# Embeddings 4 to 10 from fp16 parts, and a new order of the work that follows the embeddings, in a one-core ViT block with a routed FFN

## The reference

```python
out = jnp.einsum('bnp,dp->bnd', patches, W) + b            # patches: 768 values each
h = concatenate([cls_tok, out])                            # 37 tokens per image
h = h + attention(layernorm(h), Wq, Wk, Wv, Wo, bo, betas, mem, z)
shared = silu(x_flat @ shared_w1.T) @ shared_w2.T          # x_flat = layernorm(h)
top_k_gates, top_k_idx = jax.lax.top_k(x_flat @ gate_w.T, 2)
h = h + shared + selected                                  # selected: 2 of 8 experts, weighted
```

## Time and profile before

| | us |
|---|---|
| median of 3 runs | 326.65 (326.32 to 326.92) |
| the profiled execution's own time | 325.89 |
| its span, first to last instruction | 324.0 |
| outside the span (325.89 - 324.0) | 1.89 |
| TensorE busy | 306.7 (95%) |
| VectorE busy | 223.4 (69%) |
| ScalarE busy | 184.5 (57%) |
| GpSimd busy | 152.1 (47%) |
| mean granted TensorE clock | 0.996 of 2.4 GHz |

### The profile page before, as it was taken

One profiled execution on the slowest core, in us unless ns is written; L12 is line 12 of the kernel. 1 busy time (PEld: TensorE's weight loads), 2 busy tenths in 40 slices (PEclk: granted clock), 3 DMA queues, 4 the chain that ended last, 5 costly groups with the idle time before them and its releaser, 6 DMA issues.

```text
span 324.0 us, 9888 instructions
## 1 busy us (share of the span) xinstructions
PE 306.7 (95%) x3521; PEld 259.6 (80%) x3521; DVE 223.4 (69%) x502; ACT 184.5 (57%) x355; POOL 152.1 (47%) x208
## 2 busy tenths in 40 slices
PE   8789999999998999999999999999999999999990
PEld 6678788988777999999997777777787787777870
DVE  0637888888898989999886868755554546565530
ACT  1366768878896978476768878733232332323220
POOL 0577747777586322112622344656353544434131
PEclk9999999999999999999999999999999999999998
DMA  7775335322241117814798774243323242333121
GB/s 231 260 222 210 108 111 179 111 83 77 77 124 58 32 31 205 269 24 95 195 275 309 185 239 110 45 67 41 60 42 59 34 67 35 54 48 46 22 34 16
DMA packets 18642, 36.37 MB, mean 112 GB/s; under 512 B 3331, under 2 KB 10982, under 8 KB 18598
## 3 DMA queue, kind: packets, MB, share of 16 engines
q1 hardware_dynamic: 12166, 27.71, 26.2%
q0 software_dynamic: 6432, 8.03, 16.3%
HBM read 28.52 MB, written 7.21 MB: 110 GB/s over the span
## 4 chain that ended last, share of the span: by engine, by line
PE 76%; DVE 9%; DMA 4%; POOL 3%; issue 3%; ACT 2%; SPq 1%; POOLq 1%; DVEq 0%; ACTq 0%
PE bank L820 21%; PE bank L833 14%; PE bank L643 7%; PE bank L835 6%; PE bank L500 6%; PE bank L602 6%; DMA out_rows<-y,add_id 2%; PE bank L525 2%; PE bank L551 2%; DMA weights<-in_patches 2%; PE bank L591 2%; PE bank L565 1%; PE bank L555 1%; DVE weights L1309 1%; PE bank L453 1%
## 5 line engine op out<-in xcount | busy, mean ns | idle before, releaser
L820 PEld LDWEIGHTS bank<-x_t,weights 128*128 x1248 | 87.5, 98 | 25.5 <-issue 0.2
L820 PE MATMUL bank<-x_t,weights 128*128 128x128 f16 x1248 | 103.8, 219 | 0.0
L1002 ACT ACTIVATE act_out<-bank 128x512 f32<-128x512 f32 (+2 forms) x72 | 42.0, 585 | 86.1 <-PE bank L820 71.8
L1270 POOL DMA_INDIRECT out_rows<-y,add_id x26 | 43.0, 1653 | 69.6 <-DVE y L1626 48.1
L833 PE MATMUL bank<-weights,hid_hi 128*128 x192 | 73.3, 382 | 0.2
L1417 DVE SCALAR_TENSOR_TENSOR hid_lo<-act_out,hid_hi 128x512 f16<-128x512 f32 (+2 forms) x72 | 48.6, 680 | 12.5 <-ACT hid_hi L1013 11.0
L835 PE MATMUL bank<-weights,hid_lo 128*128 x192 | 52.3, 273 | 0.0
L1423 DVE SCALAR_TENSOR_TENSOR weights<-stage,weights 128x1024 f16<-128x1024 f32 x36 | 43.0, 1221 | 0.7 <-ACT weights L959 0.7
L959 ACT ACTIVATE weights<-stage 128x1024 f16<-128x1024 f32 x36 | 36.8, 1049 | 0.0
L1237 POOL DMA_INDIRECT slot_rows<-x_rows,gather_id x26 | 28.0, 1075 | 13.0 <-DMA out_rows<-y 5.2
L500 PE MATMUL bank<-weights 128*111 128x256 f32 x132 | 31.3, 386 | 1.6 <-DMA weights<-in_patches 1.1
(11 more groups left out here) (164 smaller groups left out, 522.8 us busy)
## 6 DMA issues: line engine op xcount, KB each, us to landing
stage<-in_w_ffn SPq DMA_DIRECT2D x36, 512.0 KB
weights<-in_patches SPq DMA_DIRECT2D x11, 333.0 KB, 3.3
x_rows<-rows SPq DMA_DIRECT2D x11, 111.0 KB
out_rows<-weights SPq DMA_DIRECT2D x10, 111.0 KB
out_rows<-y POOLq DMA_DIRECT2D x9, 119.0 KB, 5.3
weights<-in_w_embed SPq DMA_DIRECT2D x3, 256.0 KB, 4.2
stage<-in_w_qk SPq DMA_DIRECT2D x1, 512.0 KB, 6.9
slot_rows<-x_rows,gather_id POOLq DMA_INDIRECT x26, 4.1
```

Source lines behind the costliest of these rows:

```text
L820: mm = nc.tensor.matmul(o, weights[:, bass.ds(base + 2 * k * CHUNK + 2 * (col - col % D) + w * D + col % D, P)], x_t[:, b, (2 * x + k) * P ...
L1002: nc.scalar.activation(d_, s_, ACT.Silu, scale=1.0 / (X_SCALE * W_SCALE)).then_inc(hid_acted, 1)
L1270: nc.gpsimd.indirect_dma_start(out=out, out_offset=bass.IndirectOffsetOnAxis(ap=add_id[:, j:j + 1], axis=0), in_=y[:, y_place(j)], in_offs ...
```

## The change

It has two parts.

**Embeddings from fp16 parts.** From tile 4 (`F16_FROM`) on, `embed` makes 18 fp16 matmuls (three products of parts, six pieces each) in place of six float32 ones. The parts have to be made:

- of the weight, once: ScalarE writes the hi parts (128x1024 and 128x512) ahead of its other work, VectorE the lo parts in step 1;
- of the patches, for each of the tiles 4 to 10: ScalarE writes 128x666 hi values (`split_patches_hi`, at the end of the steps 1 to 6, two of them in step 2), VectorE 128x666 lo values (`split_patches_lo`, in steps 1 and 2 late in the step, in steps 3 to 7 right behind `split_lo`).

`embed_h` scales the sum back in the instruction that adds the bias. The SP queue's loads of patches now wait for the split in place of the embedding. In steps 5 to 10 VectorE waits, ahead of `split_lo`, for `rstd2` of the pair that GpSimd began at the end of the step before.

**The joint.** `shared_up(0, 0)` is no longer one piece of 24 matmuls but four of six, put between other work. `row_lo` of the tiles 6 and 7 moves from VectorE to GpSimd. On ScalarE `exps(10)` now stands ahead of `norm2(7)`.

The core of the diff:

```diff
             def embed(t):
-                pe.wait_ge(patches_in[t % PATCH_RING], 16 * (t // PATCH_RING + 1))
+                if t < F16_FROM:
+                    pe.wait_ge(patches_in[t % PATCH_RING], 16 * (t // PATCH_RING + 1))
+                else:
+                    pe.wait_ge(patch_lo, t - F16_FROM + 1)
+                if t == F16_FROM:
+                    pe.wait_ge(we_lo, 2)
...
+                if t >= F16_FROM:
+                    for n, (x, w) in enumerate(EMBED_PRODUCTS):
+                        for k in range(PC):
+                            we = we_front[:, k, w] if k < 4 else we_back[:, k - 4, w]
+                            mm = nc.tensor.matmul(embed_bank(t), patch_pair[t % 2][:, x, k * T:(k + 1) * T], we,
+                                                  start=(n == 0 and k == 0), stop=(n == 2 and k == PC - 1))
+                    mm.then_inc(embed_ready, 1)
+                    return
...
             project_v(NT - 1)
+            shared_up(0, 0, (0,))
             project_out(NT - 4)
+            shared_up(0, 0, (1,))
             mix_values(NT - 3)
             turn_prob(NT - 2)
-            shared_up(0, 0)
+            shared_up(0, 0, (2,))
             turn_rows(NT - 5)
+            shared_up(0, 0, (3,))
...
+            def split_patches_hi(t):
+                act.wait_ge(patches_in[t % PATCH_RING], 16 * (t // PATCH_RING + 1))
+                if t >= F16_FROM + 2:
+                    act.wait_ge(embed_ready, t - 1)
+                nc.scalar.mul(patch_pair[t % 2][:, 0], s_patch[:, t % PATCH_RING].rearrange("p a b -> p (a b)"),
+                              P_SCALE).then_inc(patch_hi, 1)
...
+                if s in (1, 2):
+                    split_patches_hi(s + 3)
+                if 2 <= s < NT - 4:
+                    split_patches_hi(s + 4)
...
+            exps(NT - 1)
             norm2(NT - 4)
-            exps(NT - 1)
...
+                if s - 5 in POOL_LATE_ROWS:
+                    row_lo(s - 5)
...
+            def split_patches_lo(t):
+                dve.wait_ge(patch_hi, t - F16_FROM + 1)
+                nc.vector.scalar_tensor_tensor(
+                    out=patch_pair[t % 2][:, 1], in0=s_patch[:, t % PATCH_RING].rearrange("p a b -> p (a b)"),
+                    scalar=P_SCALE, in1=patch_pair[t % 2][:, 0], op0=ALU.mult,
+                    op1=ALU.subtract).then_inc(patch_lo, 1)
...
+                if s == 1:
+                    we_lo_of(0, we_front, s_we[:, 0:4])
+                    we_lo_of(1, we_back, s_we[:, 4:])
...
+                if 5 <= s < NT:
+                    dve.wait_ge(rstd2, s - 4)
                 for c in chunks_at(s):
                     split_lo(c)
+                if 3 <= s < NT - 3:
+                    split_patches_lo(s + 3)
                 if s + 2 < NT:
                     embed_h(s + 2)
+                if s == 1:
+                    split_patches_lo(4)
...
-            row_lo(NT - 4)
```

59 lines of the change are left out of this document (48 added, 11 removed).

## The result

The changed kernel takes 328.43 us (median of 4 runs, 328.03 to 328.83) against 326.76 us before, measured beside it: ratio 1.0061, 95% interval 1.0048 to 1.0073. The profiled execution took 328.03 us, its span 326.1. A second, later measurement gave 328.44 and a ratio of 1.0055 (1.0038 to 1.0072). It is slower, by 0.6%.

What follows compares the result with a forecast made beforehand. TensorE was taken to bound the 8.90 us step, a GpSimd ring 0.27 us short of it. 325.89 + 1.8 (to the embeddings' end) - 0.3 (joint) = 327.4 profiled, 328.1 us median; own range 327.2 to 328.9, 8 in 10 324.6 to 329.7.

Steps and rivals of the forecast that it cites:

- the block that holds GpSimd: VectorE's weight split and the new patch split behind it, during which GpSimd stands still: 1.22 + 0.74 = 1.96 us.
- The step of 8.90: Time from one weight split to the next in steps 5 to 8, 8.90 us before; forecast to become 9.36.
- the forecast picture: Steps 5 to 8: GpSimd's operation beside both splits over 2 us, `residual` waiting 0.8, TensorE waiting about 0.9 for `row_lo`.
- the rival "in between": GpSimd's `xln_lo` goes ahead of the weight split, its bias ahead of the patch split; step 9.74, median 329.2; chance 0.12.
- the path that was forecast: Steps 5 to 8: both splits 1.96, GpSimd to `row_lo` 1.92, to `residual` 1.37, statistics 1.10, pair 2.95, signal 0.06: 9.36 us.
- The wait: VectorE waiting for `rstd2` ahead of the weight split: about 0.1 us, 0.02 plus some 0.06 for the signal.
- The rival "VectorE alone": GpSimd works beside both splits, so VectorE's list sets the step, 8.45 + 0.1 = 8.55; median 324.8; chance 0.25.
- "No change": Steady steps cost what joint and start give back: start at -0.3, joint at -0.9, sum +0.5, median 327.2; chance 0.17.
- "TensorE": TensorE stays the bound, so all 5.5 us of its fp16 gain come: 321.1; needs VectorE below 8.1; chance 0.03.
- Steps 0 to 4: Up to the end of the first `residual`'s statistics: 0.1 us later, with bounds -0.3 and +0.9.
- The joint: Split `shared_up`, `row_lo(6)` on GpSimd, `exps(10)` first: -0.3 us, most of the gain lost on ScalarE; bounds 0 and -0.9.
- the ring that passes through both engines: From VectorE's weight split over GpSimd's `row_lo`, TensorE, `residual`, statistics to the next split: 8.63 us before, forecast 9.36.

Runs made afterwards that it cites:

- the run with the scratch instruction: Kernel before plus one unused 128x666 VectorE instruction, two inputs in SBUF, behind the weight split in steps 3 to 7: 328.59 us, ratio 1.0069.
- the pair of scratch instructions: Kernel before plus an unused VectorE instruction behind the weight split, steps 3 to 7: two SBUF inputs 328.59 us (1.0069); one input, a reciprocal, 326.74 us (1.0000).
- the fourth: Kernel before with GpSimd's bias additions of tiles 9 and 10 moved into step 11: 325.79 us, ratio 1.0001.
- the kernel with the reciprocal: Kernel before plus an unused 128x110 VectorE reciprocal, one input in SBUF, behind the weight split in steps 3 to 7: 326.74 us, ratio 1.0000.

## Why the prediction came out as it did

**The sign and the size were right.** 328.1 was forecast and 328.43 measured. The step that carries both is the one that adds VectorE's new instruction to the block that holds GpSimd; the run with the scratch instruction shows it. That the median was met so closely is in part luck, as the sum below shows.

**The step of 8.90.** It grew to 9.48; 9.36 was forecast. Without the wait it is 9.39 from step 6 on, and there the forecast picture comes: a GpSimd operation of over 2 us, `residual` waiting 0.76, TensorE waiting 0.9 for `row_lo`. With the wait, that picture was wrong. It was the rival "in between" whose order came: `xln_lo` first, the bias between the splits, VectorE without a gap. That rival's price was too high: its step was put at 9.74 and is 9.48, the block 2.97 (58.52 to 61.49), not 3.18. By its path the step adds up: block 2.97, VectorE to the residual 2.44, statistics 1.09, pair 2.94 and 0.04 to the next split. So it is VectorE's list, with what GpSimd takes from it, that sets this step; the path that was forecast, from `row_lo` by TensorE to `residual` (1.37), would end 0.57 earlier than the residual came (61.99 + 1.37 = 63.36, against 63.93). I had written that GpSimd slipping in "changes nothing, since the two exclude each other"; on the time that is right within 0.12.

**The wait** was costed at about 0.1 a step. In the trace VectorE waits 0.55 in step 5 and not at all later, since its own list ends as late as the pair. 9.48 with it and 9.39 without agree with the cost all the same; the ratios, 1.0061 and 1.0081, cannot be told apart.

**The rival "VectorE alone"** (324.8) falls with the pair of scratch instructions. "No change" needed a start of -0.3 and a joint of -0.9, where +0.45 and -0.1 came. "TensorE" needed VectorE below 8.1, and VectorE's list is 8.48 without its losses.

**Steps 0 to 4 were mis-sized.** +0.1 was forecast, and the raw times seem to confirm it (44.95 against 44.84). From the third sum it is 30.24 against 29.79, +0.45: the loads hid 0.34 of it. My bounds (-0.3 to +0.9) held it. The patch splits of steps 3 and 4 are not the cause: the scratch instruction of the same form stands in the same place of these steps, and its kernel has 29.79, as before. What is left is the rest of the change in the steps 1 to 4, the making of the weight's parts and the first two patch splits among it; no run takes these apart.

**The joint was mis-sized.** -0.3 was forecast; the marks give -0.1. The reason put forward, that ScalarE's list around the table load decides, fits the runs: residual(8) is 0.7 earlier by the new joint, and the table load 0.1.

**The sum by the marks** is +0.45 (start), +1.82 (residual(0) to residual(4): 36.84 against 35.02) and -0.1, together +2.2 at the last mark. The medians give +1.7 and +1.9. Two terms missed by 0.2 and 0.35 in the same direction. So for the profiled execution 327.4 was forecast and 328.03 came, 0.6 more. The median was met within 0.3 only because 0.76 had been added from profile to median, where the changed kernel has 0.40, and 0.59 in its second measurement. The forecast's own range, 327.2 to 328.9, is also narrower than its bounds: start and joint both at their worst (+0.8 and +0.3 on the forecast) give 329.2.

**The signs that were named.** None of those of a wrong forecast came: no step under 8.9, the first residual 0.35 off from the mark, TensorE waiting in steps 5 to 8 for exponentials of ScalarE (1.7 us in four) but not for a copy, and GpSimd ending `row_lo` 3.51 after `rstd2` (58.48 to 61.99), a hair above the 3.5 that was set. Of the signs of a right one, three came: VectorE no longer waits for the embedding, the embedding takes 2.07 (39.06 to the next group of matmuls at 41.13), and TensorE waits for `row_lo`, 0.8 on average. Three did not: the splits are 9.48 apart and not 9.3 to 9.4, VectorE is never idle ahead of `residual`, and the longest GpSimd operation beside the block is 1.72, not over 2. Those three belong to the order that came only without the wait.

## What to carry to other kernels

Before giving VectorE an instruction with two inputs in SBUF, look at what GpSimd does at that place. In these kernels their times add, and the ring that passes through both engines grew by the whole instruction (8.63 by the rows, 9.39 with 0.74 more); the same time with one input was free. Look at both ends of a move: of the moves tried here three made a new meeting (0.78, 1.54, 1.75), and the fourth turned the saved time into a wait (1.28). Count the rings through an instruction's neighbours, not the busy shares: moved out of one ring, the split landed in the next. And where TensorE is made idle by such a wait, its clock may fall and the loss grows again, as it did twice with the patch split on GpSimd (granted 0.56 and 0.50).

## What was not expected of the hardware

Who goes first is not settled by the recorded starts. The Trainium skill, "SBUF — State Buffer", Who interferes with whom, says of VectorE's 2-port modes that whoever issues first gets the shared pair for the whole instruction, and in general: "Issue order, not op shape, decides who blocks." Here L1228 was recorded 0.22 ahead of the split and lost to it and to the next one as well (2.30), `combine`'s addition was recorded 0.11 ahead of GpSimd's subtraction, while `relu_q` was still running (65.27, 0.97), and lost (1.75), and in the changed kernel the two engines took turns. The traces record starts and not when an instruction was issued, so they neither confirm nor refute the page's rule; by recorded starts I have none that gives all three.

A meeting can be a toss. In step 10 of the kernel before `finish_sq` and the bias start together; VectorE won in the profile of before. In the kernel with the reciprocal it lost, though nothing differs in the code of that place:

```profile
92.28 0.98 DVE L1313 SCALAR_TENSOR_TENSOR weights<-weights 128x222 f32<-128x222 f32 x1
```

```profile
92.29 0.72 POOL L1218 TENSOR_TENSOR weights<-weights 111x256 f32<-111x256 f32 x1
```

The residual behind it then came 4.93 after the one before it (93.18 less 88.25), against 4.34 (92.59 less 88.25). That may be part of the spread between executions of one kernel; removing the meeting did not narrow it (325.34 to 328.09).
